# Radial network of the first three steps computed in the prepare stage, with three steps of gathers issued there and three stores on ScalarE's queue

## The chip, the cores and the metric

The kernel runs on one core of one Trainium2 chip. Its engines are TensorE (PE in the rows, PEld for its weight loads), VectorE (DVE), ScalarE (ACT), GpSimd (POOL) and SyncE (SP, which only issues transfers). SP, ACT and POOL each have a queue of their own for issuing DMA transfers; a `q` behind a name (SPq) stands for that. The metric is device time in microseconds (us) of one execution, the median of several runs; lower is better.

## What is computed

Two graph layers follow each other on 6250 nodes of 128 features and 106250 edges. The change lies in layer 0, an equivariant message layer:

```
emb  = exp(-0.5 * ((clip(length) - centres) / sigma) ** 2) * sqrt(8)     # 8 values for an edge
h    = silu(emb @ mlp_w0 + mlp_b0)                                       # the radial network: 64 wide
h    = silu(h @ mlp_w1 + mlp_b1)
w    = (h @ mlp_w2 + mlp_b2).reshape(-1, 4, 32)                          # four weights of 32 for an edge
ss, vv = xs[senders], xv[senders]                                        # gathered node rows
m0, m1 = w[:, 0] * ss, w[:, 1] * ss * Y1
m2, m3 = w[:, 2] * vv, w[:, 3] * dot(vv, Y1)
msg  = segment_sum(messages, receivers);  x = layernorm(x + out(msg))
```

Layer 1 (edge MLP by type, GRU-like update, layer norm) is not touched.

## The kernel before, in words

The edges are sorted by receiver and cut into 104 steps of 8 tiles of 128 edges (`STEPS`, `TPS`). The kernel is a row of blocks. Each block gives every engine a program of its own, and the next block begins only when all engines have ended theirs. The change touches the first two blocks.

**`prepare`** (lines 237 to 533) loads the inputs, builds the node table of layer 0 in DRAM (`node0`), the radial embedding `emb` of all edges, which stays in SBUF in the region of `acc` and is stored to DRAM for later (16 stores, line 337), the edge directions `y`, and the index lists `p_idx`, `q_idx` and `key_row` for layer 1, which are stored too (lines 341 to 344). POOL stores the node table (L419) and then gathers the sender rows of the first four steps, one slot of `gx` for each (`SLOTS` = 4, `gather_step`, eight indirect transfers a step, L549). VectorE ends with clearing a part of `acc` (L506), for which it waits until the store of `key_row` has landed (`row_st`), since the region holds that list.

**`edges0`** (from line 623) runs the 104 steps as a software pipeline, written out by hand as loops over four steps. For step j TensorE multiplies `emb` by `w0` (`first`, L837), ScalarE applies silu (L747), TensorE multiplies by `w1` (`second`, L841), ScalarE applies silu again, and TensorE makes the weights `ps_w` (`third`, L575 and L577). VectorE forms the messages from `ps_w` and the gathered rows (`vy` L598, `ws` L595, `msg` L601 and L604), ScalarE a part of them (L616), and TensorE sums them by receiver with a one-hot matrix (`sums`, L849, twice a step). `third` runs one step ahead of the messages, `second` two and `first` three. The pipeline is filled ahead of the loop by seven calls on TensorE: first, second, third of step 0, first and second of step 1, first of step 2.

SP keeps the buffers filled in this order in each step: `load_emb` (L667), which waits for the count of finished `first` calls (`h1_mm`), then the index list of four steps ahead (L663), which waits until this step's gather has landed, and, from the fourth group of steps on, node rows and stores of the table for layer 1. POOL's gather of step j+4 waits for that index list and for `used`, which VectorE raises when it is done with the slot.

## Time and profile before

| | us |
|---|---|
| median of 3 runs | 3151.82 |
| lowest and highest run | 3148.94 and 3176.6 |
| the profiled execution | 3156.88 |
| its span, first to last instruction | 3155.2 |
| its busy time: TensorE, GpSimd, VectorE, ScalarE | 2120.1, 1609.8, 1477.7, 1326.8 |

The profiled execution lies 5.06 us above the median of the runs. A row of the timeline gives the start and the length of an instruction or of a few merged ones (x2 is two records), in us from the start of the span; in brackets stand the idle time of the engine just before it and what ended that. A float32 matmul leaves two records. The stages in order of time: `prepare` to about 98.5 us, `edges0` from 101.9 to about 1600 us, then layer 1.

### The profile page before, as it was taken

To read this page: it belongs to the slowest core of one execution; us is meant where nothing else is said; L and a number is where in the kernel's file an instruction comes from. 1 tells how busy PE (TensorE), PEld (TensorE's weight loads), DVE (VectorE), ACT (ScalarE), POOL (GpSimd) and SP (SyncE) were. 2 spreads that over 40 slices of the span, in tenths; PEclk is the share of its full clock that TensorE was granted. 3 is DMA by queue.
4 is the path that set the end of the run, shared out by engine and by line. 5 is a ranking of instruction groups with operands and counts; after the bars stand their busy time and mean duration, and the time that the engine had idled before them with its cause. 6 is when DMAs were issued, how large, how long until landed. Compare 5 with 4: busy or idle time off the path is not lost. (4 is left out here: it accounts for less than half of the span.)

```text
span 3155.2 us, 43900 instructions
## 1 busy us (share of the span) xinstructions
PE 2120.1 (67%) x10012; PEld 1630.4 (52%) x10012; DVE 1477.7 (47%) x3700; ACT 1326.8 (42%) x4413; POOL 1609.8 (51%) x1699
## 2 busy tenths in 40 slices
PE   5577888778787887878845655656555656565555
PEld 3355555555555555555624544545545645555444
DVE  5334434343433443434423435646555646465556
ACT  3255545555555565555613323333323333333332
POOL 4454555555555455554233455555545555555451
PEclk6677888888888788888858777777767767777677
DMA  6311212222222122221135443333333433333331
GB/s 188 86 42 38 56 50 61 53 59 52 52 60 57 48 61 53 62 57 48 46 100 141 130 108 81 84 88 83 85 80 77 97 76 89 79 89 83 74 85 41
DMA packets 222533, 236.66 MB, mean 75 GB/s; under 512 B 73191, under 2 KB 163471, under 8 KB 222349
## 3 DMA queue, kind: packets, MB, share of 16 engines
q0 software_dynamic: 53808, 112.80, 15.5%
q10 hardware_dynamic: 90192, 57.89, 7.2%
q1 hardware_dynamic: 78493, 65.53, 7.0%
q8 instruction: 14, 0.23, 0.0%
q14 instruction: 26, 0.21, 0.0%
HBM read 191.73 MB, written 44.31 MB: 75 GB/s over the span
## 5 line engine op out<-in xcount | busy, mean ns | idle before, releaser
L549 POOL DMA_INDIRECT gx<-node_d,idx x832 | 802.2, 964 | 684.3 <-DVEq L1041 410.7
L549 POOL DMA_INDIRECT gp<-p_tab_d,idx x832 | 790.1, 950 | 692.2 <-DMA idx<-p_idx_d 405.4
L849 PEld LDWEIGHTS ps_a<-hot,msg 128*128 128x128 f32 x3328 | 489.3, 230 | 252.8 <-issue 233.5
L849 PE MATMUL ps_a<-hot,msg 128*128 128x128 f32 x3328 | 521.7, 319 | 93.8 <-issue 53.1
L616 ACT ACTIVATE msg<-ws,y 128x32 f32<-128x32 f32 x2496 | 549.7, 310 | 5.4 <-DVE ws L595 4.1
L1669 PE MATMUL ps_e<-win,hot_x 128*128 128x129 f32 x1680 | 333.5, 370 | 272.2 <-DVE hid L1812 130.5
L1669 PEld LDWEIGHTS ps_e<-win,hot_x 128*128 128x128 f32 x1680 | 302.1, 274 | 297.0 <-issue 151.6
L1733 PE MATMUL ps_g<-hot,hid 128*128 128x128 f32 x1664 | 255.1, 307 | 105.8 <-issue 102.7
L1777 DVE TENSOR_TENSOR hot_x<-key_row,ps_s 128x1024 f32<-128x1024 bf16 x106 | 128.8, 1216 | 401.0 <-remote 360.8
L747 ACT ACTIVATE h<-ps_h,b 128x512 f32<-128x512 f32 x208 | 141.8, 682 | 401.0 <-remote 265.3
L1733 PEld LDWEIGHTS ps_g<-hot,hid 128*128 128x128 f32 x1664 | 244.7, 222 | 122.3 <-issue 115.6
L577 PE MATMUL ps_w<-w,h 128*128 128x256 f32 x832 | 254.8, 448 | 47.7 <-issue 47.2
L595 DVE TENSOR_TENSOR ws<-ps_w,gx 128x256 f32<-128x256 f32 x104 | 44.1, 424 | 509.8 <-remote 403.7
L1580 ACT ACTIVATE hid<-hid,score 128x128 f32<-128x128 f32 x832 | 277.4, 392 | 10.1
L577 PEld LDWEIGHTS ps_w<-w,h 128*128 128x128 f32 x832 | 173.1, 219 | 132.2 <-issue 109.3
L962 DVE TENSOR_TENSOR acc<-acc,ps_a 128x256 f32 x104 | 43.9, 422 | 343.5 <-remote 238.6
L1812 DVE TENSOR_TENSOR hid<-ps_e,gp 128x387 f32<-128x387 f32 (+1 forms) x312 | 142.7, 508 | 114.7 <-remote 58.4
L1576 ACT ACTIVATE score<-hid 128x3 f32<-128x3 f32 (+1 forms) x312 | 60.4, 193 | 295.1 <-DVE hid L1812 215.4
L837 PE MATMUL ps_h<-emb,w 16*128 16x512 f32 x208 | 138.5, 749 | 54.2 <-ACT h L747 27.0
L841 PE MATMUL ps_h<-h,w 128*128 128x512 f32 x208 | 123.5, 679 | 30.0 <-ACT h L747 23.2
L1739 PE MATMUL ps_s<-hot_n,sc 128*128 128x128 f32 x416 | 82.3, 321 | 78.9 <-DVE sc L1825 46.8
L1785 DVE TENSOR_TENSOR hot<-ps_s,key 128x1024 f32<-128x1024 f32 x105 | 127.5, 1214 | 3.5 <-issue 3.5
(210 smaller groups left out, 2477.9 us busy)
## 6 DMA issues: line engine op xcount, KB each, us to landing
win<-q_tab_d ACTq DMA_DIRECT2D x416, 64.5 KB
key_row<-key_row_d ACTq DMA_DIRECT2D x102, 256.0 KB
gx<-node_d,idx POOLq DMA_INDIRECT x832
gp<-p_tab_d,idx POOLq DMA_INDIRECT x832
q_tab_d<-unit_area SPq DMA_DIRECT2D x51, 258.0 KB
p_tab_d<-acc SPq DMA_DIRECT2D x23, 516.0 KB
emb<-emb_d SPq DMA_DIRECT2D x104, 32.0 KB
gx<-in_x_t ACTq DMA_DIRECT2D x7, 448.0 KB, 7.0
```

The source lines that it names most:

```text
L549: e.indirect_dma_start(out=buf[:, h, t, :], out_offset=None, in_=table, in_offset=bass.IndirectOffsetOnAxis(ap=idx[:, h, t:t + 1], axis=0) ...
L577: last = e.matmul(ps_w[:, 2 * t:2 * t + 2, :], h2[:, t * P:(t + 1) * P], w["w2"][:], start=False, stop=t % 2 == 1)
L616: last = e.activation(self.cols[1][:, tile, c, :], self.ws[:, tile, :], ACT.Copy, scale=y[:, c:c + 1])
L747: e.activation(out[:], ps_h[:], ACT.Silu, bias=bias[:]).then_inc(ok, 1)
L837: e.matmul(ps_h[:], w["w0"][:], emb[:, h, :], start=True, stop=True).then_inc(h1_mm, 1)
L849: last = e.matmul(ps_a[:, h, b, :], msgs[h].tile(t, b), hot[:, h, t, :], start=t == 0, stop=t == TPS - 1)
L1580: last = e.activation(hid[:, h, t, 0:H], hid[:, h, t, 0:H], ACT.Relu, scale=score[:, h, t:t + 1])
L1669: last = e.matmul(ps_e[:, q, at:at + PW], hot_x[:, h, t, :], win[:, h, t // 2, :], start=True, stop=True)
L1733: e.matmul(ps_g[:, h, t // 2, :], hid[:, h, t, 0:H], hot[:, h, t, :], start=t % 2 == 0, stop=t % 2 == 1)
L1777: e.tensor_tensor(hot_x[:, h].rearrange("p t n -> p (t n)"), key_row[:, h, :], part.to_broadcast([P, TPS * P]), ALU.is_equal).then_inc(hx_ ...
L1785: e.tensor_tensor(hot[:, h], spread(iota[:, 0:P], 1, TPS), spread(k["key"][:, tiles], 2, P), ALU.is_equal).then_inc(hot_ok, 1)
L1812: e.tensor_tensor(hid[:, h, mine, :], ps_e[:, q, 0:n * PW].rearrange("p (t n) -> p t n", t=n), gp[:, u, mine, :], ALU.add).then_inc(pre_ok, 1)
```

## The change

The buffers and semaphores of the radial network (`h1`, `h2`, `ps_h`, `ps_x`, `ps_w`) are allocated ahead of `prepare` and live through both blocks; `prepare` uses the same PSUM banks for its own matmuls. The seven filling calls of TensorE and the four silus of ScalarE stand in `prepare`, where `first` reads `emb` straight from SBUF. Before them TensorE waits for both networks' weights, all squares, all node rows and the first half of the exponentials. POOL gathers three steps in `prepare` and the fourth at the start of `edges0`. ScalarE issues the stores of `p_idx`, `q_idx` and `key_row`. SP stores one more row of zeros behind `emb`, begins `edges0` with the embeddings of steps 3 and 4, and in step j loads that of step j+5 once `first` of step j+3 has run. On VectorE nothing is added but one wait on an instruction before (`q_idx`) and a signal. The new helpers are the old inner functions under other names:

```python
def layer0_silu(e, w, mlp, layer, value):
    mm, ok = (mlp["h1_mm"], mlp["h1_ok"]) if layer == 1 else (mlp["h2_mm"], mlp["h2_ok"])
    e.wait_ge(mm, value)
    e.activation(mlp[f"h{layer}"][:], mlp["ps_h"][:], ACT.Silu, bias=w[f"b{layer - 1}"][:]).then_inc(ok, 1)
```

```diff
@@ prepare, sync queue @@
-                e.wait_ge(row_ok, 1)
-                e.dma_start(dram["key_row"], key_r).then_inc(row_st, 16)
-                e.wait_ge(idx_ok, 1)
-                e.dma_start(dram["p_idx"], p_idx).then_inc(stored, 16)
-                e.dma_start(dram["q_idx"], q_idx).then_inc(stored, 16)
-                e.wait_ge(stored, 16 * 2)
+                e.dma_start(dram["emb"][STEPS], k["zero"][0:2 * NB, :]).then_inc(stored, 16)
+                e.wait_ge(stored, 16 * 3)
@@ prepare, scalar @@
                     e.activation(emb[:, span], emb[:, span], ACT.Exp, scale=-0.5).then_inc(exp_ok, 1)
+                e.preload_act_table(ACT.Silu)
+                layer0_silu(e, w, mlp, 1, 1)
+                layer0_silu(e, w, mlp, 2, 1)
+                e.wait_ge(idx_ok, 1)
+                e.dma_start(dram["p_idx"], p_idx).then_inc(stored, 16)
+                e.dma_start(dram["q_idx"], q_idx).then_inc(stored, 16)
+                layer0_silu(e, w, mlp, 1, 2)
+                layer0_silu(e, w, mlp, 2, 2)
+                e.wait_ge(row_ok, 1)
+                e.dma_start(dram["key_row"], key_r).then_inc(row_st, 16)
@@ prepare, gpsimd @@
-                for u in range(SLOTS):
+                for u in range(SLOTS - 1):
                     e.wait_ge(w["idx_in"][u], 16)
                     e.sem_inc(gate, 1)
                     gather_step(e, w["idx"], dram["node0"], w["gx"], w["landed"], u)
@@ prepare, tensor @@
                 in_order(node_rows, widen)
+                def first(j):
+                    e.matmul(mlp["ps_h"][:], w["w0"][:], emb[0:2 * NB, j * HALF:(j + 1) * HALF], start=True, stop=True)\
+                        .then_inc(mlp["h1_mm"], 1)
+
+                e.wait_ge(mlp_ok, 1)
+                e.wait_ge(s_own, SPC)
+                e.wait_ge(tab_ok, NG)
+                e.wait_ge(exp_ok, 1)
+                first(0)
+                layer0_second(e, w, mlp, 1)
+                layer0_third(e, w, mlp, 0, 1)
+                first(1)
+                layer0_second(e, w, mlp, 2)
+                e.wait_ge(mlp["h2_ok"], 2)
+                first(2)
                 e.wait_ge(hits_ok, 1)
@@ edges0, sync queue @@
                 def load_emb(j, h):
-                    e.wait_ge(h1_mm, j + 1)
-                    e.dma_start(emb[:, h, :], dram["emb"][bass.ds(j + 2, 1)].rearrange("s r n -> (s r) n"))\
+                    e.wait_ge(h1_mm, j + 4)
+                    e.dma_start(emb[:, h, :], dram["emb"][bass.ds(j + 5, 1)].rearrange("s r n -> (s r) n"))\
                         .then_inc(emb_in[h], 16)
...
-                        if not last or u < SLOTS - 2:
-                            load_emb(i * SLOTS + u, u % 2)
+                        if not last:
+                            load_emb(i * SLOTS + u, 1 - u % 2)
...
-                    e.dma_start(emb[:, h, :], dram["emb"][h]).then_inc(emb_in[h], 16)
+                    e.dma_start(emb[:, 1 - h, :], dram["emb"][h + 3]).then_inc(emb_in[1 - h], 16)
@@ edges0, gpsimd @@
+                e.wait_ge(idx_in[SLOTS - 1], 16)
+                e.sem_inc(gate, 1)
+                gather_step(e, idx, dram["node0"], gx, landed, SLOTS - 1)
                 gather_loop(e, idx, idx_in, dram["node0"], gx, landed, used, gate, first=1)
@@ edges0, scalar @@
                 e.preload_act_table(ACT.Silu)
-                for n in range(2):
-                    silu(h1, w["b0"], h1_mm, h1_ok, n + 1)
-                    silu(h2, w["b1"], h2_mm, h2_ok, n + 1)
@@ edges0, tensor @@
-                            first(1 - h, i * (16 * SLOTS // 2) + 16 * ((u + 3) // 2 + 1))
-
-                first(0, 16)
-                second(1)
-                third(0, 1)
-                first(1, 16)
-                second(2)
-                e.wait_ge(h2_ok, 2)
-                first(0, 32)
+                            first(1 - h, i * (16 * SLOTS // 2) + 16 * (u // 2 + 1))
+
```

TensorE, the border between the two blocks, before (L527 is `prepare`'s last large matmul, L300 and L833 are the border; `x7` is seven in a row):

```order
L527 MATMUL ps_b<-acc,of_row 128x512 x7
L533 MATMUL ps_n<-n_hit,one 1x2
L300 UNCONDITIONAL_BRANCH
L833 UNCONDITIONAL_BRANCH
L837 MATMUL ps_h<-emb,w 128x512
L841 MATMUL ps_h<-h,w 128x512
L575 MATMUL ps_w<-b,ones 128x512 x2
L577 MATMUL ps_w<-w,h 128x256 x4
L837 MATMUL ps_h<-emb,w 128x512
L841 MATMUL ps_h<-h,w 128x512
L837 MATMUL ps_h<-emb,w 128x512
L926 UNCONDITIONAL_BRANCH
```

The same place with the change (L569, L186, L626 and L628 are first, second and third; L329 and L878 the border; L886 is `sums`):

```order
L563 MATMUL ps_h<-acc,of_row 128x512
L569 MATMUL ps_h<-acc,w 128x512
L186 MATMUL ps_h<-h,w 128x512
L626 MATMUL ps_w<-b,ones 128x512 x2
L628 MATMUL ps_w<-w,h 128x256 x4
L569 MATMUL ps_h<-acc,w 128x512
L186 MATMUL ps_h<-h,w 128x512
L569 MATMUL ps_h<-acc,w 128x512
L584 MATMUL ps_n<-n_hit,one 1x2
L329 UNCONDITIONAL_BRANCH
L878 UNCONDITIONAL_BRANCH
L956 UNCONDITIONAL_BRANCH
```

All filling matmuls stand ahead of the border, and behind it comes the loop with `sums` as its first work.

GpSimd, the end of `prepare` and the start of `edges0`, before (one row with a wait and one of seven for each step of gathers):

```order
L549 DMA gx<-node_d,idx 128x128 [waits idx_in2]
L549 DMA gx<-node_d,idx 128x128 x7
L549 DMA gx<-node_d,idx 128x128 [waits idx_in3]
L549 DMA gx<-node_d,idx 128x128 x7
L300 UNCONDITIONAL_BRANCH
L739 UNCONDITIONAL_BRANCH [waits barrier_Pool_Activation_PE_DVE_SP_gather]
```

And with the change:

```order
L600 DMA gx<-node_d,idx 128x128 [waits idx_in2]
L600 DMA gx<-node_d,idx 128x128 x7
L329 UNCONDITIONAL_BRANCH
L788 UNCONDITIONAL_BRANCH [waits barrier_Pool_Activation_PE_DVE_SP_gather]
L600 DMA gx<-node_d,idx 128x128 [waits idx_in3]
L600 DMA gx<-node_d,idx 128x128 x7
```

The eight gathers of the fourth step moved behind the border.

## Rows read from the trace of the kernel before

**Rows 1.** Page: TensorE busy time; gathers of layer 0 (busy, mean ns, idle, releaser).
```profile
PE 2120.1 (67%) x10012; PEld 1630.4 (52%) x10012; DVE 1477.7 (47%) x3700; ACT 1326.8 (42%) x4413; POOL 1609.8 (51%) x1699
...
L549 POOL DMA_INDIRECT gx<-node_d,idx x832 | 802.2, 964 | 684.3 <-DVEq L1041 410.7
```

**Rows 2.** Windows: per stretch, busy time of engines, granted clock, DMA share, GB/s.
```profile
core 0: us, PE busy (x) PEld busy (x) DVE busy (x) ACT busy (x) POOL busy (x), PEclk, DMA share, GB/s
64.00:84.00 20.00, 0.19 (x2) 0.09 (x2) 19.47 (x18) 4.52 (x2) 16.04 (x14) 0.50 0.81 199
84.00:92.00 8.00, 0.00 (x0) 0.00 (x0) 0.55 (x1) 0.00 (x0) 6.17 (x7) 0.50 0.79 214
...
98.60:101.90 3.30, 0.00 (x0) 0.00 (x0) 0.00 (x0) 0.00 (x0) 0.00 (x0) 0.50 0.08 20
101.90:130.00 28.10, 23.11 (x46) 11.61 (x47) 7.31 (x11) 9.69 (x30) 7.56 (x8) 0.50 0.32 84
```

**Rows 3.** Timeline, end of prepare: start us, length us, engine, line, operation.
```profile
62.67 5.84 ACT L385 ACTIVATE acc<-acc 128x3072 f32<-128x3072 f32 x2
...
65.46 17.37 SPq L337 DMA_DIRECT2D emb_d<-acc  x16
...
72.61 1.03 DVE L486 SCALAR_TENSOR_TENSOR dst_i<-dstf,typef 128x848 uint32<-128x848 f32 x1
...
75.14 1.22 DVE L494 SCALAR_TENSOR_TENSOR acc<-acc 106x1024 bf16<-106x1024 f32 x1
...
82.87 0.30 SPq L341 DMA_DIRECT2D key_row_d<-acc  x1
...
87.55 0.95 POOL L549 DMA_INDIRECT gx<-node_d,idx  x1 [0.30 <-issue]
...
92.12 3.58 DVE L506 MEMSET acc<- 128x4228 f32 x1 [7.57 <-issue]
...
97.55 0.94 POOL L549 DMA_INDIRECT gx<-node_d,idx  x1 [0.31 <-issue]
102.02 1.28 ACT L815 ACT_TABLE_LOAD   x1 [33.50 <-PEq L300]
```

**Rows 4.** Timeline, first step of edges0, same columns.
```profile
103.76 0.95 DVE L598 TENSOR_TENSOR vy<-gx,y 128x768 f32<-128x768 f32 x1
...
103.77 2.07 PE L837 MATMUL ps_h<-emb,w 16*128 16x512 f32 x2 [20.75 <-DMA emb<-emb_d]
...
105.88 0.69 ACT L747 ACTIVATE h<-ps_h,b 128x512 f32<-128x512 f32 x1 [2.58 <-PE ps_h L837]
...
114.25 0.42 DVE L595 TENSOR_TENSOR ws<-ps_w,gx 128x256 f32<-128x256 f32 x1 [9.54 <-PE ps_w L577]
...
114.92 0.94 DVE L604 TENSOR_TENSOR msg<-ps_w,gx 128x768 f32<-128x768 f32 x1
...
116.51 0.35 SPq L663 DMA_DIRECT2D idx<-in_src  x1
...
119.16 0.94 POOL L549 DMA_INDIRECT gx<-node_d,idx  x1 [20.66 <-DMA idx<-in_src]
...
121.84 3.78 PE L849 MATMUL ps_a<-hot,msg 128*128 128x128 f32 x16
...
126.52 3.74 PE L577 MATMUL ps_w<-w,h 128*128 128x256 f32 x8
...
130.69 0.43 DVE L595 TENSOR_TENSOR ws<-ps_w,gx 128x256 f32<-128x256 f32 x1 [11.57 <-PE ps_w L577]
```

**Rows 5.** Timeline, pace of later steps of edges0, same columns.
```profile
803.35 0.42 DVE L595 TENSOR_TENSOR ws<-ps_w,gx 128x256 f32<-128x256 f32 x1 [8.07 <-remote]
...
809.83 1.99 PE L577 MATMUL ps_w<-w,h 128*128 128x256 f32 x8
...
820.33 2.07 PE L837 MATMUL ps_h<-emb,w 16*128 16x512 f32 x2
...
860.03 0.41 DVE L595 TENSOR_TENSOR ws<-ps_w,gx 128x256 f32<-128x256 f32 x1
```

More of the change, by code:

```diff
@@ L143, in build @@
                 w = layer0_weights(nc, Mem(nc, layer0))
-                prepare(nc, a, k, dram, dict(w, b2_1=later["b2"]))
                 nodes = node_views(k, later)
-                edges0(nc, a, k, dram, w, later, nodes)
+                with ExitStack() as until_leftover0:
+                    mlp = first_mlp(Mem(nc, until_leftover0))
+                    prepare(nc, a, k, dram, dict(w, b2_1=later["b2"]), mlp)
+                    edges0(nc, a, k, dram, w, later, nodes, mlp)
                 leftover0(nc, a, k, dram, w, nodes)
@@ L443, in _ @@
                 own.did(e.memset(one[:], 1.0))
-                e.memset(w["ones"][:], 1.0)
+                own.did(e.memset(w["ones"][:], 1.0))
                 e.wait_ge(ld_dst, 16)
@@ L485, in _ @@
                 own.did(e.scalar_tensor_tensor(p_idx, src_i[:], float(T), k["typef"][:], ALU.mult, ALU.add))
-                own.did(e.scalar_tensor_tensor(q_idx, dstf[:], float(T), k["typef"][:], ALU.mult, ALU.add))
+                own.then(e.scalar_tensor_tensor(q_idx, dstf[:], float(T), k["typef"][:], ALU.mult, ALU.add))
                 e.sem_inc(idx_ok, 1)
@@ L620, in tile, with edges0 @@
         return self.msg[:, b, t * H:(t + 1) * H]
-def edges0(nc, a, k, dram, w, later, v):
+def edges0(nc, a, k, dram, w, later, v, mlp):
     with ExitStack() as ctx:
```

56 lines of the change are left out of this document (30 added, 26 removed).

## Prediction, made before the changed kernel was run

> **What bounds the kernel now.** I read the page first. TensorE is busy 2120 us of a span of 3155.2 us, and the gathers of layer 0 take 802.2 us of work and 684.3 us of idle time before them for 832 transfers [rows 1]. That is 1486.5 / 832 = 1.79 us a transfer, or 14.3 us for a step of eight. POOL's own part of it is 8 x 1.25 us = 10.0 us (87.55 to 97.55 is eight of them at even spacing [rows 3]); it waits for VectorE, and VectorE waits for TensorE. So in the 104 steps of `edges0` neither the gathers nor the transfers set the pace, and the change leaves the work of TensorE, ScalarE and VectorE within a step as it was. What it can win lies at the border of the two blocks.
>
> The windows show that border. From 64 to 92 us TensorE works 0.19 us in all, at a granted clock of 0.50, the lower of the two levels (1.2 GHz); from 98.6 to 101.9 no engine is busy at all, and then TensorE works 23.1 of 28.1 us, still at the lower clock [rows 2]. The timeline tells who is late. The last gather of `prepare` starts at 97.55 and ends at 98.5; VectorE's last large instruction ends at 92.12 + 3.58 = 95.7; `edges0` starts with ScalarE's table load at 102.02 [rows 3]. So POOL ends `prepare`, 2.8 us behind VectorE, and the border itself costs about 3.4 us (98.5 to 101.9). Inside `edges0` VectorE has its first product (`vy`) at 104.71 and then sits idle 9.54 us until TensorE has the weights of step 0; TensorE in turn does second and first of the next steps before the first `sums` at 121.84, and the weights of step 1 reach VectorE at 130.69 [rows 4].
>
> **The change, part by part.**
>
> *The filling calls leave `edges0`.* VectorE then runs `vy` to 104.71 and goes straight on with `ws` and the two products behind it. In the row of before these take from 114.25 to 114.92 + 0.94 = 115.86, 1.6 us [rows 4], so the first `sums` can start at about 106.4 instead of 121.84: 15.4 us earlier against the border. All that follows on TensorE (3.78 us of `sums`, 3.74 us of `third` at the lower clock) comes after it as before, so the weights of step 1 should move from 130.69 by the same 15.4 us.
>
> *The same calls in `prepare`.* They can start when the first exponentials are done: half of the 5.84 us from 62.67, so about 65.6. ScalarE ends the other half at 68.5 and loads silu's table, 1.28 us [rows 3], so that the first silu is at 69.8 against 105.88 in the trace of before, 36.1 us earlier. The chain from that silu to the end of the third `first` is the one that stands ahead of 121.84 [rows 4], so it ends at about 121.9 - 36.1 = 85.8. This costs nothing: TensorE is idle until then and beyond [rows 2], and ScalarE has nothing after its exponentials. The count matmul queued behind it on TensorE (L533, for VectorE's very last instruction) moves from 83 to 86, in front of VectorE's clearing, which runs to 95.7 before. The cover is the 12 us from 85.8 to 98.
>
> *One step of gathers leaves `prepare`.* Eight times 1.25 us: POOL ends at 88.5 instead of 98.5 [rows 3]. The stall then passes to the next late engine, VectorE, at 95.7, and to SP, which waits for all stores. VectorE is late because its clearing waits from 84.55 (92.12 less 7.57 of idle time) to 92.12 for the store of `key_row`, issued at 82.87 behind 16 stores of `emb` on SP's queue [rows 3].
>
> *ScalarE issues three stores.* `p_idx` and `q_idx` are ready at 72.61 + 1.03 = 73.6 and go out then, between the silus of step 0 and 1; `key_row` is ready at 76.4 but queued behind four silus, so it goes out at about 84, some 1 us later than before [rows 3]. The 16 engines are 0.8 busy at about 200 GB/s from 64 to 92 [rows 2], and the bytes stay the same but for 32 KB of zeros. If the list lands as late as before, VectorE ends at 95.7 and the border moves by 2.8 us. If it overtakes the `emb` stores, as it has a queue with nothing left ahead of it, and lands at 89, VectorE ends at 92.5; then SP, whose stores of `emb` fill the engines until about 92, ends it at 92.5 to 94, a move of 4.5 to 6. I take 4.0 us, between. The Trainium skill speaks for the smaller one: its page "DMA: Bandwidth & Descriptors", section "Issuing engines are not separate DMA queues", says that transfers of all issuing engines run interleaved on the same 16 DMA engines and that a second issuer saves only issue time. By that alone the move would be 2.8 us, and the sum below 18.2. The 3.4 us of the border itself are kept; they may be partly POOL's own tail, and then up to 3 us more could go.
>
> *The moved gathers.* POOL issues them in the first 10 us of `edges0`, while it sat idle 20.66 us before [rows 4]. They have landed some 13 us after the border; VectorE wants them with step 3, and by 130.69, 29 us behind the border, it had only come to step 1 [rows 4]; less the 15.4 us that is still 13 us for step 1 alone. Cost: nothing.
>
> *SP waits later.* `load_emb` of step j now waits for `first` of step j+3, the last thing TensorE does in step j, and the index list of step j+4 is queued behind it, and with it the gather of that step; node rows and table stores too. In the steady state: step 48 has its `ws` at 803.35, `first` of step 51 ends at 820.33 + 2.07 = 822.4, and step 52 has its `ws` at 860.03 [rows 5]. With 0.7 us of issue, 2.65 us until POOL can start (116.51 to 119.16 [rows 4]), 10.0 us of gathers and as much as 2.65 us again for landing, the rows are there at 838.4, 21 us before they are wanted at about 859. The stores behind the wait are wanted two steps or more later. Cost: nothing, and the limit is this 21 us.
>
> Sum: 15.4 + 4.0 = 19.4 us. On the profiled execution that is 3156.9 - 19.4 = 3137.5 us; on the median of the runs, 5 us lower, 3151.8 - 19.4 = **3132.4 us**, which I forecast.
>
> **The rivals.**
>
> *The gain is given back by TensorE's clock.* Before, TensorE worked nearly without pause from 103.77 on and was granted the lower clock until 130 [rows 2, 4]. With the change it starts from rest at about 98 + 4.5. If the clock rises as late after that start as it did before, some pieces more run slow: a `third` takes 3.74 us at the lower clock and 1.99 at the higher [rows 4, 5], and I estimate the same 1.7 us for each of the others, which have as many columns in all. With five or six pieces that is 9 to 10 us, and the time is about 3141. In the worst case the whole head start is used up: 3150. For it: four later steps take 860.03 - 803.35 = 56.7 us, 14.2 each [rows 5], while the page has TensorE busy only 67% of the span [rows 1], so its pace is not made of its recorded work alone. Against it: a lower clock at the start was there before too.
>
> *The pace of the 104 steps shifts.* What stretches the steps to 14.2 us is not explained by the rows. The change moves the gathers in time against TensorE's work by some 17 us (from about 805.5, when the products behind 803.35 are done, to 822.4), and with them POOL's and the DMA engines' load. If the pace changes by 0.15 us a step beyond the gain, that is 15 us either way; by 0.4 us, 40 us: 3092 or 3173.
>
> *The later wait on SP starves the gathers.* This is the one that ends slower. It decides where a step's rows land more than 21 us later than worked out, for instance if SP is held by another wait before it comes to `load_emb`. Each step then takes as long as the chain of `first`, index list and gather; with 0.5 us a step, 100 steps and the gain of 19 us it gives 3183, with 1 us 3233. For it: all of SP's work is in one order. Against it: its other waits in a step (x1, its transpose, the table) end before `first` of that step.
>
> *The change does not do what it says*, because the border is set by SP's stores and these end later: then only the 15.4 us stay, less a few: 3138. This lies within the forecast's own range.
>
> **How the numbers follow.** The forecast, a gain of 12 to 30 us (3122 to 3140): 0.66. The clock gives back (3140 to 3152): 0.13. The pace shifts to the better by more than 10 us beyond the gain (below 3122): 0.09, and to the worse: 0.06. The gathers starve: 0.06. For 8 in 10 the range reaches from 3118 to 3152. Since about 1% (31.5 us, below 3120.3 or above 3183.3) is what a measurement can tell from no change, faster by over 1% has 0.10, nearly all of it a shift of the pace; slower by over 1% has 0.05, from the starved gathers and a worse pace; within 1% has 0.85.
>
> **What would show it.** The last gather of `prepare` ends at 88 to 89; VectorE's clearing starts at 89 to 92; `edges0` starts at 96 to 99.5; the first `sums` follows 4.5 us later and the weights of step 1 another 9 us later, at about 111. POOL then idles on the index list instead of on VectorE, and VectorE never waits on a gather. I am wrong if VectorE shows waits for `gx`, if the granted clock stays low past 20 us after the border, or if the mean step of `edges0` is not 14.2 us.

## The result, and the profile after

The changed kernel takes 3212.28 us (median of 4 runs, 3202.32 to 3228.78), the kernel before on the same chip 3159.15 us (median of 4 runs, 3148.94 to 3176.60). The ratio is 1.0175, with a 95% interval of 1.0131 to 1.0219: slower by 53 us, where 19 us less were forecast. The profiled execution of the changed kernel is the longest of its runs, 3228.78 us with a span of 3227.1.

First the page of the changed kernel: TensorE's total, the gathers of layer 0 and VectorE's first product of each step, `ws`, which starts when TensorE has delivered the step's weights (busy us, mean ns | idle us before, and what ended most of it).

```profile
PE 2115.3 (66%) x10012; PEld 1615.1 (50%) x10012; DVE 1477.2 (46%) x3700; ACT 1333.4 (41%) x4414; POOL 1611.0 (50%) x1699
...
L600 POOL DMA_INDIRECT gx<-node_d,idx x832 | 802.8, 965 | 757.9 <-DMA idx<-in_src 468.1
...
L646 DVE TENSOR_TENSOR ws<-ps_w,gx 128x256 f32<-128x256 f32 x104 | 43.9, 423 | 577.2 <-remote 434.4
```

The groups of costliest lines of the kernel before have the same product:

```profile
L595 DVE TENSOR_TENSOR ws<-ps_w,gx 128x256 f32<-128x256 f32 x104 | 44.1, 424 | 509.8 <-remote 403.7 <-PE ps_w L577 85.3 <-issue 20.5
```

All engines do what they did [rows 1]. Idle time grew: 73.6 us in front of the gathers, now ended by their index lists instead of by VectorE, and 67.4 us in front of `ws`. Most of the latter is "remote" in both kernels: when the wait ended, no instruction in the trace had just ended that could have released it. That word is the clue to what follows.

The border of the two blocks moved as forecast. Windows of the changed kernel, the columns as in [rows 2]:

```profile
core 0: us, PE busy (x) PEld busy (x) DVE busy (x) ACT busy (x) POOL busy (x), PEclk, DMA share, GB/s
64.00:84.00 20.00, 13.82 (x19) 5.13 (x20) 19.16 (x18) 7.86 (x7) 16.42 (x12) 0.50 0.86 218
84.00:92.00 8.00, 1.30 (x4) 0.09 (x2) 0.00 (x0) 0.00 (x0) 3.82 (x5) 0.50 0.65 156
92.00:102.00 10.00, 0.00 (x0) 0.00 (x0) 6.16 (x6) 1.28 (x1) 1.89 (x2) 0.50 0.07 19
102.00:120.00 18.00, 16.48 (x71) 12.37 (x72) 9.80 (x17) 12.77 (x52) 6.96 (x7) 0.70 0.45 118
```

and its timeline (start us, length us, engine, line, operation, idle time before it), with the answers to [rows 3, 4]:

```profile
82.37 0.50 ACTq L420 DMA_DIRECT2D key_row_d<-acc  x1
...
83.11 2.07 PE L569 MATMUL ps_h<-acc,w 16*128 16x512 f32 x2 [0.78 <-issue]
...
88.10 0.94 POOL L600 DMA_INDIRECT gx<-node_d,idx  x1 [0.30 <-issue]
95.03 3.58 DVE L542 MEMSET acc<- 128x4228 f32 x1 [11.18 <-DMA key_row_d<-acc]
...
98.89 1.28 ACT L863 ACT_TABLE_LOAD   x1 [15.84 <-PEq L329]
99.62 0.95 POOL L600 DMA_INDIRECT gx<-node_d,idx  x1 [10.58 <-POOLq L329]
...
100.99 0.95 DVE L649 TENSOR_TENSOR vy<-gx,y 128x768 f32<-128x768 f32 x1
101.85 0.42 DVE L646 TENSOR_TENSOR ws<-ps_w,gx 128x256 f32<-128x256 f32 x1
...
103.52 3.78 PE L886 MATMUL ps_a<-hot,msg 128*128 128x128 f32 x16 [18.22 <-issue]
```

TensorE's filling calls now lie in the 20 us in which it had been idle, the last of them at 83.11; POOL ends `prepare` at 89.0 instead of 98.5; `ws` follows `vy` without a wait; the first `sums` is at 103.52 (121.84 before). The second `ws` is at 112.01 us (130.69 before). So step 1 begins 18.7 us earlier, and the forecast of 19.4 holds up to there.

It is lost in the loop. From the first `ws` (101.85) to the 104th (1615.90) there are 1514.1 us, before 1454.0 (114.25 to 1568.25). Between the second and the 103rd, the mean step is 14.83 us, before 14.17: 0.66 us times 101 steps is 67 us, and 67 less 19 is 48 us, nearly all of the 53 between the medians. (The two profiled spans differ by 72 us. The other 24 lie behind the 104th `ws`, in the second layer, which the change does not touch: 1611.2 against 1586.9 us there, while the eleven other kernels below that leave this layer alone show 1565.6 to 1608.8. No verdict is built on these 24 us.)

Who waits longer in the loop? SyncE's waits at `load_emb`, from the table of waits (total us, times, longest): of the changed kernel

```profile
SPq L716 <- PE ps_h L882: 596.5, 50, 22.3
SPq L716 <- remote: 495.0, 43, 14.3
```

and of the kernel before

```profile
SPq L667 <- remote: 136.8, 14, 21.4
SPq L667 <- PE ps_h L837: 69.2, 10, 11.0
```

SyncE stood there 206 us before and stands there 1091.5 us now, and the index lists are queued behind it. Yet VectorE never waits for a gather's rows in either trace. The lists and gathers are late, and no engine waits for them: the lateness itself is not the loss. The timeline shows what is. Around 803 us in the kernel before (`third` of the next step is the row at 809.83 in [rows 5]):

```profile
805.81 0.94 POOL L549 DMA_INDIRECT gx<-node_d,idx  x1 [4.37 <-DVEq L1041]
...
813.37 1.95 PE L849 MATMUL ps_a<-hot,msg 128*128 128x128 f32 x16
814.56 0.94 POOL L549 DMA_INDIRECT gx<-node_d,idx  x1 [0.30 <-issue]
816.57 0.42 DVE L595 TENSOR_TENSOR ws<-ps_w,gx 128x256 f32<-128x256 f32 x1 [7.21 <-remote]
817.29 0.39 ACT L788 ACTIVATE acc<-ps_x 128x258 f32<-128x258 f32 x1 [7.28 <-remote]
```

`third` is recorded as ended at 811.82, but VectorE goes on 4.75 us later, 1.07 us after POOL's run of eight gathers ends at 815.50. ScalarE, which waits for another matmul (`ps_x`), is held at the same place. In this trace 64 of the 104 steps have `ws` more than 2 us behind the recorded end of `third`; in 61 of them that end lies inside an unbroken run of gathers, and 49 start within 2.5 us after the end of such a run. (Runs of gathers cover 0.68 of the loop's time, so by chance some 44 of the 64 would end in one.) Now the changed kernel at the same place:

```profile
816.48 1.08 POOL L600 DMA_INDIRECT gx<-node_d,idx  x1 [5.17 <-DMA idx<-in_src]
...
822.97 1.99 PE L628 MATMUL ps_w<-w,h 128*128 128x256 f32 x8
823.77 0.69 ACT L181 ACTIVATE h<-ps_h,b 128x512 f32<-128x512 f32 x1 [3.41 <-remote]
823.92 0.33 SPq L716 DMA_DIRECT2D emb<-emb_d  x1
...
827.14 1.15 PE L886 MATMUL ps_a<-hot,msg 128*128 128x128 f32 x6 [1.32 <-issue]
827.84 0.94 POOL L600 DMA_INDIRECT gx<-node_d,idx  x1 [1.52 <-issue]
...
830.98 1.09 PE L886 MATMUL ps_a<-hot,msg 128*128 128x128 f32 x2 [0.86 <-issue]
...
836.58 0.95 POOL L600 DMA_INDIRECT gx<-node_d,idx  x1 [0.30 <-issue]
839.54 0.42 DVE L646 TENSOR_TENSOR ws<-ps_w,gx 128x256 f32<-128x256 f32 x1 [12.23 <-remote]
839.58 0.69 ACT L181 ACTIVATE h<-ps_h,b 128x512 f32<-128x512 f32 x1 [12.59 <-remote]
```

SyncE is released for `load_emb` in the middle of a run (823.92). The index list behind it is fetched in time for the next eight gathers to follow the first eight after a gap of 1.52 us: sixteen from 816.48 to 837.53. TensorE's `sums` come out in pieces with gaps; VectorE and ScalarE stand for 12 us and start 2.0 us after the last gather. The weights that VectorE wants (`third`) are recorded as ended at 824.96, and it was ready for them at 827.32, in that gap: 1.52 us let nothing through. That step takes 22.9 us (816.66 to 839.54).

Which hand-overs are late? The waits of VectorE, ScalarE and SyncE that end with "remote" are waits for TensorE: VectorE waits for `ps_w` and `ps_a`, ScalarE for `ps_h` and `ps_x`, SyncE for the count of `first`. Hand-overs the other way can be prompt. In the kernel before, inside a run of gathers that goes from 835.86 to 854.32:

```profile
837.23 0.67 ACT L747 ACTIVATE h<-ps_h,b 128x512 f32<-128x512 f32 x1
...
837.95 1.12 PE L841 MATMUL ps_h<-h,w 128*128 128x512 f32 x2 [0.71 <-ACT h L747]
```

TensorE starts 0.05 us after ScalarE ends, and where TensorE stands idle for this silu inside a run it is 0.05 us each time: 49 of 49 cases in before, after, p_pause, q_best and r_both. It is not always so on the way into TensorE: its `sums` start up to 8.3 us behind the last of ScalarE's messages (changed kernel). The recorded end of a matmul is modelled, so the rows do not tell whether TensorE's signal is late or TensorE itself.

When in a run does it begin? I took every `third` that is recorded as ended inside a run, and what passes from then, or from the moment at which VectorE is free, to `ws`. In the changed kernel 34 end in the first 5.2 us of their run, and none is taken up more than 0.5 us late; 37 end later than 6 us into it, and 33 of these are late, by 10.7 us on the mean of the 37. In the kernel before it is 8 of 13 (none of the five in the first 3.7 us) and 47 of 53, by 3.4 us. So the changed kernel has fewer late hand-overs and longer ones: where two steps of gathers follow each other, a held `third` waits for the end of both.

I counted the runs in every trace that has gathers in the loop: POOL's runs of gathers (gaps under 0.6 us, after 110 us), the long ones of more than nine, the steps of 18 us or more, the mean step, and the mean of the others that are under 18 us (steps from the second `ws` on).

| kernel | runs | long runs | slow steps | mean step, us | mean of the others, us |
|---|---|---|---|---|---|
| before | 96 | 12 | 18 | 14.17 | 12.68 |
| after | 80 | 24 | 29 | 14.83 | 11.39 |
| a3_early_idx | 89 | 13 | 19 | 14.22 | 12.59 |
| b3_late_gather | 91 | 16 | 17 | 13.07 | 11.42 |
| f_both | 95 | 11 | 16 | 13.02 | 11.46 |
| g_late_idx | 84 | 23 | 29 | 14.53 | 11.57 |
| h_halves | 110 | 29 | 11 | 13.68 | 12.88 |
| p_pause | 101 | 0 | 0 | 11.90 | 11.86 |
| q_best | 105 | 0 | 2 | 12.29 | 12.07 |
| q_short | 178 | 0 | 17 | 13.87 | 12.44 |
| e_sp_stores | 78 | 24 | 29 | 14.82 | 11.53 |
| r_both | 100 | 0 | 0 | 12.00 | 11.96 |

The change makes the ordinary step 1.3 us shorter and doubles the number of long runs; 24 of its 29 slow steps overlap one (11 of 18 before). The step shown above is one of the other five, for its gap of 1.52 us. If a gap of up to 1.7 us is counted as part of a run, the long runs are 19 before and 30 after, and every slow step overlaps one: 18 of 18 and 29 of 29 (of all 103 steps 38 and 46 do).

### The profile page after: what moved, and what is told of

Same layout as the page of the kernel before. It is cut to its first block and busy times, and to the rows that moved or that the text cites. A ratio compares the mean times of both kernels' runs of the same rounds, so it can differ in the third digit from the quotient of the medians.

```text
span 3227.1 us, 43901 instructions
## 1 busy us (share of the span) xinstructions
PE 2115.3 (66%) x10012; PEld 1615.1 (50%) x10012; DVE 1477.2 (46%) x3700; ACT 1333.4 (41%) x4414; POOL 1611.0 (50%) x1699
## 3 DMA queue, kind: packets, MB, share of 16 engines
q0 software_dynamic: 53808, 112.80, 15.2%
## 5 line engine op out<-in xcount | busy, mean ns | idle before, releaser
L886 PEld LDWEIGHTS ps_a<-hot,msg 128*128 128x128 f32 x3328 | 493.6, 229 | 439.9 <-issue 436.3
L886 PE MATMUL ps_a<-hot,msg 128*128 128x128 f32 x3328 | 540.8, 321 | 263.8 <-issue 126.8
L667 ACT ACTIVATE msg<-ws,y 128x32 f32<-128x32 f32 x2496 | 552.0, 309 | 22.1 <-issue 21.5
L628 PE MATMUL ps_w<-w,h 128*128 128x256 f32 x832 | 233.0, 426 | 4.5 <-issue 4.1
L628 PEld LDWEIGHTS ps_w<-w,h 128*128 128x128 f32 x832 | 163.6, 207 | 78.0 <-issue 57.2
L186 PE MATMUL ps_h<-h,w 128*128 128x512 f32 x208 | 112.3, 623 | 26.4 <-ACT h L181 23.2
```

Of the source, the lines that this page charges most:

```text
L628: last = e.matmul(ps_w[:, 2 * t:2 * t + 2, :], h2[:, t * P:(t + 1) * P], w["w2"][:], start=False, stop=t % 2 == 1)
L667: last = e.activation(self.cols[1][:, tile, c, :], self.ws[:, tile, :], ACT.Copy, scale=y[:, c:c + 1])
L886: last = e.matmul(ps_a[:, h, b, :], msgs[h].tile(t, b), hot[:, h, t, :], start=t == 0, stop=t == TPS - 1)
```

## The experiments

The expectations number the theories in the order in which they arose. The first says that the moved `load_emb` wait on SyncE makes the index lists and gathers late, and that lateness costs the time; its rival puts the loss elsewhere in the change or in the DMA traffic. The second blames ScalarE's stores. The third, on record together with the first, says that signals are held up while GpSimd issues gathers without a break; its first wording has TensorE's signals, the later ones those of "the other engines", which is more than the traces show. The fourth says that gathers which wait for the index list run into each other. Each run has its own runs of the kernel before beside it; ratios are against these. "Before" or "after" in a diff's heading is the kernel that is edited.

### SyncE's order undone

After, with `load_emb` as it was:

```diff
 def load_emb(j, h):
-    e.wait_ge(h1_mm, j + 4)
-    e.dma_start(emb[:, h, :], dram["emb"][bass.ds(j + 5, 1)]...
+    e.wait_ge(h1_mm, j + 1)
+    e.dma_start(emb[:, h, :], dram["emb"][bass.ds(j + 2, 1)]...
```

> The changed kernel with one part undone: in step j SyncE again loads the embedding of step j+2 and waits for first of step j (the first three steps of the loop load none), so that the index list behind it, and with it the gather, can go out as early as before the change. Filling calls in prepare, three steps of gathers there and ScalarE's stores stay. Theory 1 (the later wait on SyncE moved the gathers, and this lengthened the steps from 14.1 to 14.7 us): the mean step is 14.1 us again, the head start of 12 to 19 us stays, total 3130 to 3145. Rival 2 (the work of TensorE in prepare, the clock, or other addresses of the buffers): the steps stay at 14.7 us and the total at about 3210.

Measured: 3124.3 us (12 runs) against 3141.5, a little below the 3130 to 3145 expected; ratio 0.9944 (0.9913 to 0.9975), a gain of 17 us. The mean step is 14.22 us again, with 13 long runs. All else in the change, moved work and ScalarE's stores, gives what was forecast for the whole: 17.2 us against 19.4. The whole loss comes with the wait that had been costed at nothing.

### The gather made late, without SyncE

Before, where POOL's gather of step j+4 also waits until `first` of step j+3 is done, the same late moment as in the change:

```diff
...
     e.wait_ge(used, i * SLOTS + (u + 1))
...
+    e.wait_ge(h1_mm, i * SLOTS + u)
     gather_step(e, idx, dram["node0"], gx, landed, u)
```

> The kernel before with one wait added: GpSimd's gather of step j+4 also waits for first of step j+3 on TensorE, as it does through SyncE in the changed kernel. Nothing else is changed. Theory 1: the mean step rises from 14.1 to 14.5 to 14.9 us and the total to 3200 to 3240. Rival 2: nothing moves, 3150 to 3165, since the rows are on hand 20 us before they are wanted.

Measured: 3028.9 us; ratio 0.9645 (0.9603 to 0.9687), mean step 13.07. The first theory fell here: it wanted a loss of 2 or 3%, and the later gather is a gain of 3.5%. The ordinary steps have the 11.4 us of the changed kernel, and the long runs stay few, 16. The idle time in front of `ws` fell from 509.8 to 348.1 us:

```profile
L595 DVE TENSOR_TENSOR ws<-ps_w,gx 128x256 f32<-128x256 f32 x104 | 43.9, 422 | 348.1 <-remote 222.6 <-issue 88.7 <-PE ps_w L577 36.7
```

### No gathers, and the same bytes issued by SyncE

Two kernels that tell GpSimd's issuing from the traffic. In the first, POOL only signals that rows have landed, from step 4 on; the gathers of the loop are left out, and products use old rows. In the second, SyncE issues plain transfers of the same size, eight a step, from fixed rows in place of the gathered ones.

```diff
-gather_loop(e, idx, idx_in, dram["node0"], gx, landed, used, gate, first=1)
...
+    e.wait_ge(used, i * SLOTS + (u + 1))
...
+    e.sem_inc(landed[u], 16 * TPS)
```
```diff
...
 load_idx(i * SLOTS + (u + SLOTS), u)
+e.wait_ge(used, i * SLOTS + (u + 1 + SLOTS))
...
+for t in range(TPS):
+    e.dma_start(gx[:, u, t, :], dram["node0"][t * P:(t + 1) * P, :]).then_inc(landed[u], 16)
```

> The kernel before without the gathers inside the loop of layer 0: steps 4 to 103 use the rows of steps 0 to 3 again (this part of the computation is left out), and the signal of a landed gather is given at once. Theory 3 (while GpSimd issues gathers in one unbroken run, signals of TensorE arrive late, and that makes the step 14.1 us): the mean step falls to 7 to 10 us, total 2450 to 2750. Rival (TensorE's own work or its clock sets the step): the step stays at 13 to 14.1 us and the total within 100 us of 3155.

> The kernel before with the gathers inside the loop of layer 0 replaced by as many plain transfers of the same size and row length (128 rows of 512 bytes), issued by SyncE at the same signal; the rows are not those of the senders (this part of the computation is left out). If GpSimd's own issuing is what holds the others: the mean step is 7 to 11 us as without gathers. If it is the traffic of the rows: 13 to 14.5 us.

Measured: 2691.1 us without gathers (ratio 0.8569, 0.8515 to 0.8623), 2685.1 us with plain transfers (0.855, 0.849 to 0.861), two runs each; mean step 9.59 and 9.60 us. The windows from 140 to 1000 us: of the kernel before,

```profile
140.00:1000.00 860.00, 677.56 (x3026) 473.81 (x3025) 345.80 (x699) 447.48 (x1668) 463.82 (x483) 0.82 0.20 53
```

and with SyncE's transfers:

```profile
140.00:1000.00 860.00, 826.96 (x4555) 592.39 (x4553) 518.56 (x1050) 677.72 (x2504) 0.00 (x0) 0.99 0.28 80
```

The second moves 80 GB/s where the kernel before moves 53, and is faster by 456 us. So the traffic is not what stretches the steps; GpSimd's gathers are. No run has GpSimd issue plain transfers, so whether it is GpSimd's issuing as such or the indirect form was not tested. In front of `ws` nothing is "remote" any more, and all idle time ends with the matmuls that feed it. Without gathers:

```profile
L595 DVE TENSOR_TENSOR ws<-ps_w,gx 128x256 f32<-128x256 f32 x104 | 44.2, 425 | 231.1 <-PE ps_w L577 231.1
```

and in its timeline `ws` starts 0.05 us after the recorded end of `third` (805.35 + 1.99), where it was 4.75 us above:

```profile
805.35 1.99 PE L577 MATMUL ps_w<-w,h 128*128 128x256 f32 x8
...
807.39 0.42 DVE L595 TENSOR_TENSOR ws<-ps_w,gx 128x256 f32<-128x256 f32 x1 [2.69 <-PE ps_w L577]
```

### Both edits, and SyncE's order alone

The changed kernel with the first two edits together:

> The changed kernel with two edits: SyncE's order undone as in the run before (a3), and GpSimd's gather of step j+4 waits for first of step j+3, as in b3. If the two gains come from different places (12 to 19 us at the border, 112 us from the shorter steps) they add up: 3141 - 112 - 17 = 3012, between 2995 and 3025, and the mean step is 13.1 us. If the head start in TensorE's work disturbs the gathers' place in the step, the mean step is back at 14 and the total above 3090.

Measured: 3018.8 us; ratio 0.9603 (0.9559 to 0.9648), mean step 13.02. The head start and the pace add up (2995 to 3025 was expected for that), so they are two separate things.

The counterpart: before, with nothing of the change but SyncE's order. `emb` is loaded one step earlier, and the index list of step j+4 waits for `first` of step j+3:

```diff
...
+e.sem_inc(gate_x, 1)
+e.wait_ge(h1_mm, i * SLOTS + (u + 4))
 load_idx(i * SLOTS + (u + SLOTS), u)
```

> The kernel before with SyncE's order of the changed kernel alone: the index list of step j+4 is loaded only after first of step j+3 (the embedding of step j+3 is loaded one step earlier, so that nothing locks). Filling calls, gathers in prepare and stores as before. Theory 4 (gathers held until the index list lands, 3 us after first, run into each other: more unbroken runs of 16 gathers, each of which holds the other engines some 20 us): mean step 14.6 to 14.9 us, 24 or more runs of 16 instead of 12, total 3190 to 3235. Rival (late gathers are good wherever they wait, as in b3): mean step 13 to 13.5 us, total 3030 to 3080. Rival 2 (it was the work moved to prepare after all): 3135 to 3165.

Measured: 3187.2 us; ratio 1.0147 (1.0097 to 1.0197), a loss of 38 us between the medians, just below the range expected, as are the mean step, 14.53 us, and the 23 long runs. There are 29 slow steps; the changed kernel has 24 and 29. This order alone makes the double runs. The same wait, put on SyncE ahead of the list, loses 1.5%, and on POOL behind the list gains 3.5%. The two differ in what happens behind the wait: on SyncE the list still has to be fetched, so that the gathers start some 2.65 us later behind `first` [rows 4]. In both the ordinary steps are short (11.6 and 11.4 us); it is the number of long runs, 23 against 16, and of slow steps, 29 against 17, that differs. Why the one order makes more of them was not tested.

### The eight gathers divided by a wait

Before, where the last four gathers of a step wait for ScalarE's signal `y_ok` of step j:

```diff
...
 for t in range(TPS):
+    if t == TPS // 2:
+        e.wait_ge(y_ok, i * SLOTS + (u - 3))
+        e.sem_inc(gate, 1)
     e.indirect_dma_start(...
```

> The kernel before with each step's eight gathers cut in two: the last four of step j+4 wait until ScalarE has finished its messages of step j. Theory 3 (what holds the other engines is an unbroken run of gathers of more than some 6 us): a run of four ends before it holds anybody, the mean step falls to 10 to 12.5 us and the total to 2750 to 2980. If the number of gathers in a step counts, not the run: the step stays at 14 us and the total within 40 us of before.

Measured: 3096.0 us; ratio 0.9826 (0.9766 to 0.9886), mean step 13.68. It missed its range by over 100 us. The trace suggests why: the wait did not always break the run (31 runs still have eight gathers), and sometimes it put the second half of one step directly in front of the next, so that 29 runs of twelve or sixteen came about. A wait that may already be met is no sure break.

### A break that is always there

So the break was made from GpSimd's own work: a memset of 128x1536 that nobody needs, and a wait for it, in the middle of each eight gathers of the first layer.

```diff
...
 for t in range(TPS):
+    if t == TPS // 2:
+        e.memset(rest[:], 0.0).then_inc(rested, 1)
+        e.wait_ge(rested, i * SLOTS + (u - 3))
+        e.sem_inc(gate, 1)
     e.indirect_dma_start(...
```

> The kernel before with a pause of GpSimd of 1.5 to 2 us (a memset of a scratch tile and a wait for it) in the middle of each eight gathers, which otherwise go out as before. Theory 3: the pause ends the run, the others catch up in it, the mean step falls below 13 us and the total below 3040. If only GpSimd's total time counts: each step grows by the pause, 16 us, and the total by 150 to 200 us.

Measured: 2930.3 us; ratio 0.9302 (0.9247 to 0.9357). The kernel before with 100 useless memsets of 1.40 us is 7% faster. The mean step is 11.90 us; no run has more than eight gathers and no step takes 18 us. Runs of eight are still the rule (99 of 101), four gathers of one step and four of the next: what is gone are the long ones. The costliest lines of its POOL and the row of `ws`:

```profile
L753 POOL DMA_INDIRECT gx<-node_d,idx x800 | 781.9, 977 | 312.3 <-issue 260.1 <-POOL rest L750 31.4 <-DMA idx<-in_src 20.7
L750 POOL MEMSET rest<- 128x1536 f32 x100 | 139.7, 1397 | 0.0
...
L595 DVE TENSOR_TENSOR ws<-ps_w,gx 128x256 f32<-128x256 f32 x104 | 43.8, 422 | 255.3 <-remote 174.9 <-PE ps_w L577 74.1 <-issue 6.3
```

The row of the gathers also shows the next bound: GpSimd itself. Of the 312.3 us in front of them, 20.7 are a wait for an index list, once, at the start; all else is its own pace and its own memset. From one memset to the next it takes 12.13 us on the mean ((1327.13 - 126.03) / 99), 12.26 in q_best and 12.11 in r_both below. VectorE now waits 16 times for gathered rows in this loop, 25.7 us in all, where it never did before.

How long must the break be? And does the changed kernel's head start stay? Two kernels, both the changed one with SyncE's order undone and a break in each eight gathers: of 128x1536, and of 128x128.

> The changed kernel with SyncE's order of the transfers of `emb` undone (as in a3_early_idx) and with GpSimd's memset of 128x1536 (1.40 us in p_pause) and the wait for it between the fourth and the fifth gather of each step of the first layer. Nothing is left out. Theory 3 (it is the unbroken run of gathers that holds up the signals of the other engines; the filling calls' gain is apart from it): 2930.3 us of p_pause less the 17.2 us that a3_early_idx gained = 2913, between 2900 and 2928, with `ws` in the trace at 102 and 112 us, a mean step under 12.2 us and no run of more than nine gathers. Rival, the steps' pace goes back to where another engine sets it and the head start is taken back by a wait in the loop: 2930 as p_pause.

> q_best with a memset of 128x128 in place of 128x1536: the break in the run of eight gathers becomes some 0.2 to 0.4 us of work and the wait for it, in place of 1.4 us. If a break of any length, with GpSimd's instruction stream waiting once, lets the other engines' signals through: 2900 to 2925, as q_best or a little less. If it takes a break of the length of the hold that is seen at a run's end (1 to 2 us): nearer to a3_early_idx, 3050 to 3130, with steps of 18 us and more again. Nothing is left out.

Measured: 2962.6 us for the long break (ratio 0.9342, 0.9278 to 0.9406), 3111.4 us for the short one (0.9847, 0.9802 to 0.9891). The short break is 0.22 us of work (100 memsets, 22.2 us) and 0.78 us until the next gather, and it gives 13.87 us a step, where none at all gives 14.22 (a3_early_idx): that the instruction stream waits once is not enough. With the memset of 1.40 us and the same 0.78 us, it is 12.29 us. This is seen directly in the long one's timeline; here four gathers of one step and four of the next follow each other without a gap, and then comes the memset:

```profile
1075.71 0.95 POOL L806 DMA_INDIRECT gx<-node_d,idx  x1 [0.30 <-issue]
1076.65 1.39 POOL L803 MEMSET rest<- 128x1536 f32 x1
1078.51 0.42 DVE L646 TENSOR_TENSOR ws<-ps_w,gx 128x256 f32<-128x256 f32 x1 [8.06 <-remote]
1078.56 0.39 ACT L852 ACTIVATE acc<-ps_x 128x258 f32<-128x258 f32 x1 [8.48 <-remote]
1078.83 0.95 POOL L806 DMA_INDIRECT gx<-node_d,idx  x1 [0.78 <-issue]
```

VectorE and ScalarE both go on 1.9 us after the memset's start, before the next gather. Of the `ws` that come more than 2 us behind the end of `third`, 41 of 68 start within 2.4 us of a memset's start in p_pause, 5 of 61 in q_short: most get through the long break and few through the short one. The first half of the expectation failed: q_best was to reach 2900 to 2928. The head start is there (second `ws` at 103.88 us, in p_pause at 128.83; 8.7 of these 25 us are ScalarE's exponentials, which end earlier in this execution), but the mean step is 12.29 us against 11.90, with two steps of 18.9 and 22.1 us, and the 104th `ws` comes at 1352.4 against 1338.8. The expectation took the pace of p_pause as given, and that pace is GpSimd's: its first memset is 12.9 us earlier than in p_pause, its last 0.6 us. Whether GpSimd's longer period is scatter or follows from the edits, q_best alone leaves open; r_both below, with the same first layer, keeps a lead.

### ScalarE's stores

The changed kernel with the three stores issued by SyncE again.

> The changed kernel with the three stores (p_idx, q_idx, key_row) issued by SyncE again, as before. It prices ScalarE's stores at the border: by the prediction's sum they delay the first `ws` of the loop by up to 4 us or, if ScalarE was not what it waits for, nothing; the first `ws` at 101.8 us in the changed kernel, here 98 to 102. The whole time has the slow steps of the changed kernel, 3190 to 3230. Theory 2 (ScalarE's stores, not the order of the gathers, cost the time): back to 3135.

Measured: 3172.9 us in its one run, the kernel before at 3157.6; 3190 to 3230 was expected. Its second layer is the shortest of all (1565.6 us behind the 104th `ws`, 1611.2 in the changed kernel), so the verdict goes by the loop: mean step 14.82 us and 24 long runs, as in the changed kernel. The stores are no part of the loss, and the theory that blamed them is out. The first `ws` is at 93.0 us, outside the 98 to 102 expected. For their price at the border, the whole of `prepare` has to be taken out, since the end of ScalarE's exponentials itself lies between 60.8 and 70.9 us in different executions. From that end to ScalarE's table load, which opens `edges0`, it is 28.8 us here; with ScalarE's stores 31.1, 29.9, 29.3, 28.5, 29.9 and 27.6 us in six kernels (mean 29.4); in seven kernels with the old border 33.3 to 34.5 and once 37.3 (mean 34.4). So the border moves by 5.0 us, and the second issuer has no part in it that can be seen. By the Trainium skill, page "DMA: Bandwidth & Descriptors", section "Issuing engines are not separate DMA queues", a second issuer saves no more than issue time; the traces agree.

### The break in both layers

The second layer gathers in the same way and was touched by none of these. r_both is q_best with a break there too, of three memsets of 128x480.

```diff
...
 for t in range(TPS):
+    if t == TPS // 2:
+        for r in range(3):
+            e.memset(rest[:], 0.0).then_inc(rested, 1)
+            e.wait_ge(rested, i * (3 * SLOTS) + (3 * u + r + 1))
+            e.sem_inc(gate, 1)
     e.indirect_dma_start(...
```

> q_best with a break in each eight gathers of the second layer too: three memsets of 128x480, each waited for, between the fourth and the fifth gather of a step (by the 1.40 us that 128x1536 takes, about 0.45 us each and 0.3 us for each wait, 2.3 us in all; GpSimd is busy for 794 of 1563 us there, so that 104 of them, 240 us, fit). Nothing is left out. Theory 3 (an unbroken run of gathers holds up the signals of the other engines, whatever the layer): the second layer, 1609 us from the 104th `ws` to the end in q_best, gets 4 to 8% shorter, 1480 to 1545 us, and the whole 2835 to 2900. Rival, the second layer's steps are set by other waits (its own engines are released by VectorE and ScalarE as often as by TensorE) and the break only delays its gathers: 2955 to 3000. The first layer is q_best's again: 104th `ws` at 1335 to 1360 us, by which it is seen whether the two steps of 19 and 22 us in q_best recur.

Measured: 2708.4 us (2702.4 to 2712.2) against 3147.9; ratio 0.8644 (0.8574 to 0.8713). It was expected at 2835 to 2900. It is the fastest kernel of the study that computes the whole result, 15% below the changed one by the ratios (0.8644 / 1.0175). From the 104th `ws` (1321.0 us) to the end are 1379.6 us, where q_best has 1608.8: 14% less, about twice what was expected. VectorE's first large instruction of a step in that layer, in q_best:

```profile
L1823 DVE TENSOR_TENSOR hot_x<-key_row,ps_s 128x1024 f32<-128x1024 bf16 x106 | 128.8, 1216 | 423.0 <-remote 385.0 <-PE ps_s L1785 20.2 <-issue 10.5
```

and in r_both, with the product that reads the gathered rows:

```profile
L1839 DVE TENSOR_TENSOR hot_x<-key_row,ps_s 128x1024 f32<-128x1024 bf16 x106 | 128.4, 1212 | 35.2 <-PE ps_s L1801 16.4 <-remote 9.9 <-DMA key_row<-key_row_d 6.5
...
L1874 DVE TENSOR_TENSOR hid<-ps_e,gp 128x387 f32<-128x387 f32 x208 | 107.9, 556 | 385.2 <-DMA gp<-p_tab_d,idx 329.2 <-remote 22.8 <-PE ps_e L1731 21.0
```

The "remote" 385.0 us are down to 9.9. Now VectorE waits for the gathers themselves, 329.2 us, and GpSimd waits for nobody here either (of the 316.3 us in front of its gathers in this layer, 7.7 are a wait for an index list): the bound is GpSimd's own issuing, with the breaks in it. The two steps of 19 and 22 us of q_best do not recur in the first layer (mean step 12.00). Its 104th `ws`, expected at 1335 to 1360, is 17.8 us ahead of that of p_pause; 8.9 us of this are exponentials that ended earlier.

## Why the prediction was wrong, point by point

**The filling calls leave `edges0`: right.** 15.4 us were worked out for the first `sums`; it moved from 19.8 us behind the table load (102.02 to 121.84) to 4.6 us (98.89 to 103.52), 15.2 us.

**The same calls in `prepare` cost nothing: right.** The last `first` ends at 85.18, forecast 85.8, and VectorE's clearing begins 9.9 us later.

**One step of gathers leaves, ScalarE stores, 4.0 us: right in size, in part by luck.** It is 3.1 us in this trace and 5.0 over the kernels above. The steps in between were off. `key_row` was to be issued 1 us later than before and went out 0.5 us earlier (82.37 against 82.87), and yet landed later. VectorE's clearing did not start at 89 to 92 but at 95.03, later than before. The border closed because POOL's tail went with it: from the end of VectorE's clearing to the table load it is 0.28 us now (98.61 to 98.89), where from POOL's end it had been 3.5. The prediction named this as a possibility and did not count it.

**The moved gathers cost nothing: right** as far as tested; VectorE waits for none.

**SP waits later, cost nothing: this step failed.** It compared when the rows land with when they are wanted, 21 us of slack, and that was right too: they are never waited for. What it left out is what POOL's issuing does to TensorE's hand-overs. The wait shifts the gathers against these and against each other, long runs go from 12 to 24, and each holds VectorE, ScalarE and SyncE where they wait for TensorE. Price: 0.66 us for each of 101 steps, 67 us. SyncE's order alone, in g_late_idx, costs 38 us between the medians (1.5%), and undoing it returns the kernel to a gain of 17. The mean step was among the signs of error that the prediction named ("not 14.2 us"), and it is the one that came.

**The rivals.** That "the pace of the 104 steps shifts" came true, with a chance of 0.06 on the worse side. Its own formula, with 0.66 us a step in place of the 0.4 assumed, gives 3132.4 + 67 = 3199 us for the 3212 measured. The sentence ahead of it, that the rows do not explain the 14.2 us of a step, was the warning, and the "8.07 <-remote" in [rows 5] was the row to follow: of the 64 steps of that trace with a late `ws`, 61 have the end of `third` in the middle of a run of POOL. A pace that is not explained by any engine's work is not a constant that a change leaves alone; the range of 3118 to 3152 took it for one. The rival of starving gathers had the right wait and the wrong mechanism. The clock gave nothing back: from 102 to 120 us the granted clock is 0.70 already (window above; 0.50 from 101.9 to 130 before [rows 2]), and over the loop TensorE's recorded work is 11.2 us a step in both kernels (windows in the last section: 916.76 / 1160 x 14.17 and 873.21 / 1160 x 14.83).

## What to carry to other kernels

Where GpSimd issues indirect transfers back to back, and waits for TensorE end with "remote" though its matmul had long ended by the record, lay the ends of these waits beside the ends of GpSimd's runs. If they coincide, the number of gathers in an unbroken run is a cost of its own: break the run with something that always takes its time (here a memset of 1.4 us, 2.2 us from gather to gather; a wait that may be met already, or 1.0 us from gather to gather, did little), and only then judge where to put the gathers. The break is GpSimd's own time: once GpSimd waits for nobody, it is the bound (12 us a step here, against 9.6 without gathers), and a head start elsewhere need not show. When a wait is moved that decides when gathers are issued, ask which of TensorE's hand-overs it lays into the later part of a run and whether two runs can meet, not only whether the rows are in time.

## What the runs showed of the hardware

While GpSimd issues indirect gathers 0.30 us apart, engines that wait for TensorE go on late if what they wait for ends more than some 4 to 6 us after the start of the run (changed kernel: 0 of 34 late in the first 5.2 us, 33 of 37 later than 6 us; q_best, where the runs follow a memset, has 9 of 37 late in the first 5.2 us), most often 1 to 2 us after the end of a run of eight (kernel before), and 2.5 to 3.2 us after a run of sixteen (changed kernel); some get through in the middle of one, late as well (823.77 above, 3.25 us behind the recorded end of `first`). TensorE's instructions meanwhile come out one or a few at a time. A silu of ScalarE reaches TensorE in 0.05 us inside a run (837.95 above). Plain transfers of the same size issued by SyncE do nothing of the kind (9.60 us a step, against 14.17; 1 `ws` of 104 more than 2 us behind `third`, against 64). What inside the chip holds TensorE's hand-overs no run shows. The Trainium skill, page "SBUF — State Buffer", section "SBUF: two separate sides", has one lock by which GpSimd can stop another engine: a port pair that it shares with VectorE, while ScalarE and TensorE never wait for it. By that rule VectorE alone would be late, and by its own work; here ScalarE is late by as much (12.59 us against 12.23 at 839.5 us), and both wait for TensorE, so that lock does not explain the hold.

Part of what a break gains may come by way of TensorE's clock. From 140 to 1300 us the kernel before, and then p_pause:

```profile
140.00:1300.00 1160.00, 916.76 (x4120) 643.20 (x4118) 469.20 (x950) 610.48 (x2264) 624.85 (x651) 0.83 0.20 53
```
```profile
140.00:1300.00 1160.00, 989.90 (x4970) 692.60 (x4969) 569.91 (x1146) 733.51 (x2730) 880.73 (x861) 0.93 0.24 64
```

and the changed kernel:

```profile
140.00:1300.00 1160.00, 873.21 (x3911) 607.09 (x3911) 446.30 (x905) 582.05 (x2146) 592.10 (x618) 0.81 0.19 51
```

Before and in p_pause the granted clock is 0.83 and 0.93, and TensorE's recorded work in a step goes from 11.2 to 10.2 us (916.76 / 1160 x 14.17, and 989.90 / 1160 x 11.90), 1.0 of the 2.3 us gained. Shorter waits and a higher clock come together in these windows, and no run takes them apart. For the loss of the changed kernel it plays no part, its work in a step being the same.
